# One chunk a turn by single-row DMAs, shared between SyncE and ScalarE; one-hots and a bias addition moved on VectorE

## What is computed

```python
# 6250 nodes x 256; 106250 edges sorted by target (17 per node on average)
x = x + gnn(layernorm(x))      # graph layer, LSTM-like cell, projection
x = x + ffn(layernorm(x))      # slice attention over all nodes

# gnn(z):
agg = segment_sum(z[src], dst)                       # the gather and the sum over edges
h = relu(agg @ W_rel + b_rel + z @ W_root)           # 256 -> 512
i, f, g, o = split(h @ W_ih.T + b_ih + b_hh, 4)      # 512 -> 2048, f unused
c = sigmoid(i) * tanh(g)
return (sigmoid(o) * tanh(c)) @ W_fc + b_fc          # 512 -> 256

# ffn(z): weights = softmax((z @ W_x + b_x) @ W_slice ...) per head,
# tokens = weights^T (z @ W_fx), attention among the 64 tokens of a head,
# then weights @ tokens and W_out for every node
```

## Time and profile before

| | before |
|---|---|
| median of 3 runs | 1237.53 us (1236.96 to 1239.23) |
| profiled execution | 1240.34 us, of which span 1238.5 us |
| PE busy, share of span | 1116.1 us, 90% |
| DVE | 831.8 us, 67% |
| POOL | 805.3 us, 65% |
| ACT | 627.2 us, 51% |
| granted PE clock, mean | 0.994 |

### The profile page before, as it was taken

How to read it: one execution, slowest core, us unless ns; L and a number is a source line. 1 busy time by engine, 2 the same in 40 slices (tenths; PEclk the granted TensorE clock), 3 DMA queues, 4 the chain that set the end, 5 groups by cost and what they waited for, 6 DMA issues and landing times. The chain is left out here.

```text
span 1238.5 us, 30254 instructions
## 1 busy us (share of the span) xinstructions
PE 1116.1 (90%) x9821; PEld 967.1 (78%) x9821; DVE 831.8 (67%) x2560; ACT 627.2 (51%) x1257; POOL 805.3 (65%) x856
## 2 busy tenths in 40 slices
PE   1077799999999999999999999999999999999998
PEld 0046688878888888788888787888888878897798
DVE  7885476667666766676677756775767566746665
ACT  5872444554456454545554545455545454555332
POOL 5877777777777777777777777777777777400000
PEclk9998999999999999999999999999999999999999
DMA  8674444444454445444544444444444454313498
GB/s 313 225 268 119 125 130 136 147 142 136 129 148 142 141 124 150 140 140 123 150 149 138 121 148 150 137 121 150 147 136 122 150 149 137 97 44 116 129 336 290
DMA packets 92966, 188.74 MB, mean 152 GB/s; under 512 B 20914, under 2 KB 55591, under 8 KB 92821
## 3 DMA queue, kind: packets, MB, share of 16 engines
q0 software_dynamic: 39168, 107.01, 30.0%
q1 hardware_dynamic: 42794, 59.89, 14.8%
q10 hardware_dynamic: 10859, 20.05, 4.5%
HBM read 154.87 MB, written 32.00 MB: 151 GB/s over the span
## 5 line engine op out<-in xcount | busy, mean ns | idle before, releaser
L700 POOL DMA_INDIRECT ring<-table,sidx x798 | 763.5, 957 | 247.5 <-issue 242.7
L419 PE MATMUL ps<-h_h,wih_h 128*128 128x250 f32 x1200 | 338.8, 282 | 0.0
L420 PE MATMUL ps<-h_l,wih_h 128*128 128x250 f32 x1200 | 336.5, 280 | 0.0
L421 PE MATMUL ps<-h_h,wih_l 128*128 128x250 f32 x1200 | 336.5, 280 | 0.0
L419 PEld LDWEIGHTS ps<-h_h,wih_h 128*128 128x128 f32 x1200 | 230.1, 192 | 2.0 <-issue 0.8
L420 PEld LDWEIGHTS ps<-h_l,wih_h 128*128 128x128 f32 x1200 | 230.2, 192 | 1.1
L421 PEld LDWEIGHTS ps<-h_h,wih_l 128*128 128x128 f32 x1200 | 230.1, 192 | 0.0
L850 ACT ACTIVATE gate<-ps,bgate 128x250 f32<-128x250 f32 x300 | 124.2, 467 | 140.7 <-PE ps L421 139.7
L651 DVE TENSOR_SCALAR oneh<-iota,didx 128x64 f16<-128x64 f16 (+2 forms) x1179 | 183.1, 259 | 0.0
L1078 PE MATMUL ps<-ring,oneh 128*32 128x512 f16 x2280 | 151.0, 391 | 34.5 <-DMA ring<-table,sidx 31.9
L1078 PEld LDWEIGHTS ps<-ring,oneh 128*32 128x32 f16 x2280 | 59.5, 97 | 107.7 <-DMA ring<-table,sidx 46.4
(11 more groups left out here) (213 smaller groups left out, 2508.4 us busy)
## 6 DMA issues: line engine op xcount, KB each, us to landing
sp_ring<-table SPq DMA_DIRECT2D x1920, 1.0 KB
ring<-table,sidx POOLq DMA_INDIRECT x798
swt_d<-swt ACTq DMA_DIRECT2D x25, 500.0 KB
gate<-swt_d SPq DMA_DIRECT2D x19, 500.0 KB, 5.9
x_room<-in_x SPq DMA_DIRECT2D x12, 512.0 KB, 10.6
xn<-table SPq DMA_DIRECT2D x25, 224.0 KB
xin<-in_x SPq DMA_DIRECT2D x25, 224.0 KB
res<-xin SPq DMA_DIRECT2D x25, 224.0 KB
```

The lines of the kernel that those rows point to most:

```text
L419: eng.matmul(dst, wh, xh, start=first, stop=False)
L420: eng.matmul(dst, wh, xl, start=False, stop=False)
L421: return eng.matmul(dst, wl, xh, start=False, stop=last)
L700: pool.indirect_dma_start(ring[:, j, :], None, table, bass.IndirectOffsetOnAxis(ap=idx, axis=0)).then_inc(done, 16)
```

## The change

- `SP_STEP` 52 to 33 and `SP_N` 15 to 23: chunks 86, 119, ..., 812 are fetched row by row, one a turn; GpSimd's list has 8 chunks less.
- Of such a chunk's 128 rows SP issues 88 (8, 16 and 64 a turn, 88 in turn 0; addresses in loads of 22) and ACT 40 (20 in turn 0, then 40 a turn in steady state; addresses in loads of 10). Each of the two waits for the slot and the addresses itself; PE waits for all 128 rows as before.
- ACT's rows stand at eleven places of its turn; its turns are written out one by one, no longer a hardware loop.
- DVE's one-hots for block 2t+2 are written half in turn t, where all stood, and half in turn t+1, between the statistics of `norm_x2` and the reciprocal (the new `scale_x2`).
- `add_bfc` stands right after the one-hots of block 2t+1, ahead of `cell_c` 0.

```diff
-    SP_FIRST, SP_STEP, SP_N, SP_SLOTS = 86, 52, 15, 3
+    SP_FIRST, SP_STEP, SP_N, SP_SLOTS = 86, 33, 23, 3
...
-    ROWS_FIRST, ROWS, LOADS = 96, (8, 16, 60), 32
+    ROWS_FIRST, ROWS, LOADS = 88, (8, 16, 64), 22
+    SP_ROWS = 4 * LOADS
+    ACT_ROWS = P - SP_ROWS
+    ACT_FIRST, ACT_LOADS = 20, 10
...
+        def wait_slot(eng, k):
+            if k == 0:
+                eng.wait_ge(spi_done, 1)
+            if k >= SP_SLOTS:
+                b = last_reader(SP_CHUNKS[k - SP_SLOTS])
+                eng.wait_ge(sum_done[b % 2], b // 2 + 1)
+                eng.wait_ge(sum_done[(b - 1) % 2], (b - 1) // 2 + 1)
+
+        def load_starts(eng, k, q, n):
+            _, at = nc.values_load_multi_w_load_instructions(
+                sp_idx[k:k + 1, q:q + n], engines=[eng.engine], min_val=0, max_val=(N - 1) * row_bytes,
+                skip_runtime_bounds_check_because="the DMA checks its bounds")
+            return at
+
+        def fetch_row(eng, k, q, start):
+            to = sp_ring[q:q + 1, k % SP_SLOTS, :].bitcast(U8)
+            eng.dma_start(to, rows8[ds(start, row_bytes)].rearrange("(p c) -> p c", p=1)).then_inc(
+                sp_rows[k % SP_SLOTS], 16)
...
-        def hots(eng, b):
+        def hots(eng, b, part=None):
...
+            half = len(plan) // 2
+            chunks = list(plan.items())[(part or 0) * half:half if part == 0 else len(plan)]
+            if part != 1:
+                after(eng, sum_done[e], b // 2)
...
-            last.then_inc(hot_done[e], 1)
+            if part != 0:
+                last.then_inc(hot_done[e], 1)
...
+            def load_rows():
+
+                r = loaded[0]
+                if r < last_row and r < row_at[0] + ACT_LOADS:
+                    k, q = r // ACT_ROWS, r % ACT_ROWS
+                    if q == 0:
+                        wait_slot(act, k)
+                    for i, start in enumerate(load_starts(act, k, SP_ROWS + q, ACT_LOADS)):
+                        starts[r + i] = start
+                    loaded[0] += ACT_LOADS
+
+            def fetch_rows(n):
+
+                for r in range(row_at[0], min(row_at[0] + n, loaded[0])):
+                    fetch_row(act, r // ACT_ROWS, SP_ROWS + r % ACT_ROWS, starts.pop(r))
+                    row_at[0] += 1
+
             def turn(t, odd, gather, gnn, ffn, ahead):
+                if t == 0:
+                    for _ in range(ACT_FIRST // ACT_LOADS):
+                        load_rows()
+                        fetch_rows(ACT_LOADS)
                 if gnn:
                     split_x(t - 1)
+                    load_rows()
+                    fetch_rows(9)
                     relu_h(t - 1, 0)
...
-                    gates(t - 1, 0, 4)
+                    fetch_rows(2)
+                    gates(t - 1, 0, 2)
+                    load_rows()
+                    fetch_rows(1)
+                    gates(t - 1, 2, 4)
                     tanh_c(t - 1, 0)
+                    load_rows()
+                    fetch_rows(9)
...
-                    gates(t - 1, 4, 8)
+                    gates(t - 1, 4, 6)
+                    fetch_rows(1)
+                    gates(t - 1, 6, 8)
                     tanh_c(t - 1, 1)
+                    fetch_rows(4)
                     gates(t - 1, 8, 10)
+                    load_rows()
+                    fetch_rows(3)
...
                     gates(t - 1, 10, 12)
+                    fetch_rows(1)
                     high_hl(t - 1, 0)
+                    fetch_rows(1)
                     tanh_c(t - 1, 3)
...
+                    fetch_rows(1)
                     high_hl(t - 1, 1)
...
                                   swt[:, :, :, :].rearrange("p e j n -> p (e j n)")).then_inc(swt_st, 16)
+                    fetch_rows(9)
...
-            with act.Fori(lo, hi, step) as t:
+            for t in range(lo, hi, step):
...
                     norm_x2(t - 2)
+                    if gather:
+                        hots(dve, 2 * t, 1)
+                    scale_x2(t - 2)
...
                 if gather and gnn:
                     hots(dve, 2 * t + 1)
                 if gnn:
+                    add_bfc(t - 1)
+                if gnn:
                     cell_c(t - 1, 0)
...
                 if ahead:
-                    hots(dve, 2 * t + 2)
+                    hots(dve, 2 * t + 2, 0 if t else None)
...
-                if gnn:
-                    add_bfc(t - 1)
```

More of the change, by code:

```diff
@@ L438, in out_count @@
             return 16 * (len(range(q, NCH + 1, TILES)) + (len(REST_PARTS) - 1 if q == NCH % TILES else 0))
+        rows8 = table.bitcast(U8).rearrange("n c -> (n c)")
+        row_bytes = 4 * C
+        def wait_slot(eng, k):
[14 more added lines that the diff above has]
+                sp_rows[k % SP_SLOTS], 16)
         @block.sync
@@ L517, in _ @@
             row_at = [0]
-            rows8 = table.bitcast(U8).rearrange("n c -> (n c)")
-            row_bytes = 4 * C
             def fetch_rows(n):
-                for r in range(row_at[0], min(row_at[0] + n, SP_N * P)):
-                    k, q = r // P, r % P
+                for r in range(row_at[0], min(row_at[0] + n, SP_N * SP_ROWS)):
+                    k, q = r // SP_ROWS, r % SP_ROWS
                     if q == 0:
[L526 to L531, removed]
-                    if q % LOADS == 0:
[L533 to L539, removed]
+                        wait_slot(sp, k)
+                    if q % LOADS == 0:
+                        starts[:] = load_starts(sp, k, q, LOADS)
+                    fetch_row(sp, k, q, starts[q % LOADS])
                 row_at[0] += n
@@ L548, in turn @@
                     for j, k in SP_OF.items():
-                        assert first_reader(j) // 2 > t or row_at[0] >= (k + 1) * P, (t, j, k, row_at)
+                        assert first_reader(j) // 2 > t or row_at[0] >= (k + 1) * SP_ROWS, (t, j, k, row_at)
                 if gather:
@@ L579, in _ @@
             last_turns(turn)
-            assert row_at[0] >= SP_N * P
+            assert row_at[0] >= SP_N * SP_ROWS
             def f_load(n, k):
@@ L642, in ln_low @@
                               ALU.subtract).then_inc(ln_lo[q], 1)
-        def hots(eng, b):
+        def hots(eng, b, part=None):
             e, (plan, _) = b % 2, hot_plan(b)
-            after(eng, sum_done[e], b // 2)
-            for j, (w0, w1, at) in plan.items():
+            half = len(plan) // 2
+            chunks = list(plan.items())[(part or 0) * half:half if part == 0 else len(plan)]
+            if part != 1:
+                after(eng, sum_done[e], b // 2)
+            for j, (w0, w1, at) in chunks:
                 n = WIN * (w1 - w0)
@@ L873, in copy_out @@
                                ACT.Copy).then_inc(att_a, 1)
-            def turn(t, odd, gather, gnn, ffn, ahead):
+            row_at, loaded, starts = [0], [0], {}
+            last_row = SP_N * ACT_ROWS
+            def load_rows():
[11 more added lines that the diff above has]
+                    row_at[0] += 1
+            def turn(t, odd, gather, gnn, ffn, ahead):
+                if gather and t < NP - 1:
+                    for j, k in SP_OF.items():
+                        assert first_reader(j) // 2 > t or row_at[0] >= (k + 1) * ACT_ROWS, (t, j, k, row_at)
+                if t == 0:
+                    for _ in range(ACT_FIRST // ACT_LOADS):
+                        load_rows()
+                        fetch_rows(ACT_LOADS)
                 if gnn:
                     split_x(t - 1)
+                    load_rows()
+                    fetch_rows(9)
                     relu_h(t - 1, 0)
@@ L936, in _ @@
             lo, hi, step = turns(turn)
-            with act.Fori(lo, hi, step) as t:
+            for t in range(lo, hi, step):
                 two_turns(turn, t)
             last_turns(turn)
+            assert row_at[0] == last_row
             def f_high(n, k):
@@ L1545, in norm_x2, with scale_x2 @@
                     dve.bn_aggr(mv[0:WN, 0, e, :], stats[0:WN, 0, e, :]).then_inc(var_done, 1)
+            def scale_x2(p):
                 dve.wait_ge(sd_done, p + 1)
```

## The result

The changed kernel takes **1363.46 us** (median of 4 runs, 1362.18 to 1369.3) against 1237.37 us before: a ratio of **1.1025**, 95% interval 1.0999 to 1.1051. It is 126 us slower, where 11.2 us of gain were forecast. The profiled execution took 1369.3 us around a span of 1367.5 us; its mean granted TensorE clock is 0.955 (0.994 before).

What follows compares the result with a forecast made beforehand. GpSimd's back-to-back gathers were taken as the bound, at 1.263 us each. Nine fewer before block 48 save 11.4, less up to 0.4 in the last turns: 11.2 off 1237.53 gives 1226.3 us, between 1223.5 and 1229 (chance 0.66).

Steps and rivals of the forecast that it cites:

- the price of an address load: SyncE's and ACT's register loads: between 2.13 for 32 and 0.486 for one, 22 take 1.60 and 10 take 0.96.
- The "hidden" of SyncE's 2.1 us: SyncE's queue: rows +1.3 and loads +0.8 a turn, hidden in its 4.6 us wait at L555 for the next turn.
- TensorE (B): TensorE becomes the bound as ACT's covers spill, some gain left: 1230.5, range 1229 to 1236; chance 0.14.
- contention of issuers (C): Rows issued by SyncE and ACT go one after the other: 1250; decides from ACT pitch of some 0.48; chance 0.12.
- slower gathers (D): Additional rows slow GpSimd's gathers; 1.4% (0.018 us) eats the 11.4 us, time 1235 to 1240; chance 0.08.
- The slower side: Chance that the kernel measures slower than before: 0.11, contention of issuers (C) less its edge.
- Fewer gathers, nine times 1.263: GpSimd's list: block 48 waits for the 777th gather instead of the 786th, 11.4 us less if TensorE keeps up.
- TensorE's turn of 39.3 to 40.0: TensorE's own turn: 39.28 to 39.99, taken as 39.6, under GpSimd's supply of 40.65 us a turn.
- ACT's rows: ACT's turn: 16.6 us more of rows and loads, mostly hidden in its waits; up to +0.36 a turn for TensorE.
- the last place: ACT's 9 rows behind the store: split_x 1.65 late, 1.29 covered; up to +0.36 us, nothing if the store moves ahead.
- Half of the one-hots: VectorE before softmax_end: it begins 1.9 earlier, TensorE's 0.68 wait at L1155 shrinks by 0.33 to 0.68 a turn.
- b_fc sooner, 0 to 0.3: VectorE before cell_c: 0.76 us put in a 0.84 wait, now waiting for the x load; costs 0 to 0.3.

Runs made afterwards that it cites:

- e1_aligned: The change with same rows and places, but address loads all beginning at multiples of four registers (SyncE 20, 24, 20, 24; ACT 12, 8, 12, 8): 1231.76 us, ratio 0.9942.
- e8_whole_onehots: Against e1_aligned: all one-hots of block 2t+2 written in turn t again, b_fc still added early: 1235.25 us.
- e9_rows_alone: Against e1_aligned: both VectorE edits undone (one-hots whole, b_fc at its old place), so only the rows are new: 1231.71 us.
- e2_sp_aligned: Against the change: only SyncE's loads moved to multiples of four (20, 24, 20, 24), ACT's left at 10 each: 1243.52 us, ratio 1.0036.

## Why the prediction was wrong, step by step

- **The step that failed** is the price of an address load: "on a line between, 22 take 1.60 and 10 take 0.96". The line was drawn through the number of registers. The row for 32 and the one for a single register are both of loads that begin at a multiple of four, so the trace held no load of the other kind, and two rows of one kind were taken for the bounds of both. Half of the new loads are of the other kind: 4.87 instead of 1.60. (The others were 0.25 to 0.32 too low as well, for their length; all four at 1.85 to 1.92 would still have been hidden.) SyncE's loads grew by 13.5 - 5.6 = 7.9 us a turn, not by 0.8; with 1.3 for the rows that is 9.2 against the 4.6 of slack. 41.1 + 9.2 - 4.6 = 45.7 would be the turn; 46.7 was measured, the other 1.0 in the rows and the gaps between them (30.8, where before they took 41.1 - 4.6 - 5.6 - 2.5 = 28.4 and 1.3 were to come). The kernel before showed only loads from a multiple of four on (2.13 for 32), which made 22 look cheap. The Trainium skill, Runtime: NRT & Kernel Launch, "Instruction fetch mechanics", gives some 200 ns a register for a TENSOR_LOAD, even in bulk. It speaks of loads that the runtime puts in; of these loads from SBUF, those from 2 on agree (0.200), those from a multiple of four on don't (0.056).
- **The "hidden" of SyncE's 2.1 us** stood on that price. The slack itself was read rightly, as the turn just worked out shows to within 1.0.
- **Which engine could become the bound.** The rivals had TensorE (B), contention of issuers (C) and slower gathers (D), none SyncE itself, though its slack was one subtraction away. The slower side was given 0.11 for a mechanism that the rows don't show: ACT's beside SyncE's take 0.34 to 0.37 each (9 in 3.10 to 3.36 us), far from the 0.48 from which C decides. Rival D's price had a slip: 0.018 us more a gather are 14 us over 777 gathers; 0.0147 (1.2%) would eat the 11.4.

```profile
660.15 3.36 ACTq L462 DMA_DIRECT2D sp_ring<-table  x9
...
666.17 3.10 ACTq L462 DMA_DIRECT2D sp_ring<-table  x9
```

- **Fewer gathers, nine times 1.263.** Right in kind, as e1_aligned shows. The chain again goes from GpSimd to TensorE at block 48:

```profile
1044.20 0.94 POOL ring L719
...
1045.45 2.74 DMA ring<-table,sidx
...
1048.23 0.61 PE ps L1143 x7
```

  The 777th gather is issued at 1045.45, 7.9 us before the 786th of before. Nine gathers are 11.4; the first starts 1.7 earlier (60.59); and 776 gathers at 1.2692 instead of 1.2626 cost 5.1, rival D on a small scale. Part of these 5.1 may be no effect of the change, as profiles with the gathers of the kernel before range from 1.263 to 1.269. With aligned loads the forecast was right save for this term: 7 to 8 us of gain where 11.2 were forecast.
- **TensorE's turn of 39.3 to 40.0.** Right for aligned loads: TensorE's stalls for gathers, 37.6 us in 25 places, remain in a mean turn of 40.8.
- **ACT's rows** were covered place by place as said once the loads were short: TensorE's wait for the last split is 3.2 us in all. It was the earlier store, from the halved one-hots, that covered the last place, as the step said: with whole one-hots this wait is 14.4 in 22 places (e8_whole_onehots) and 9.3 in 20 (e9_rows_alone). With 3.7 us a turn more on ACT the covers do not hold (e2_sp_aligned); they were as thin as rival B had them.
- **Half of the one-hots**: right (1.3 in 2 places instead of 16.3 in 24).
- **b_fc sooner, 0 to 0.3.** Right with aligned loads as to the wait: VectorE waits for the x load only once at the start and once at the end (5.4 us in 2 places). In the change itself the new place costs 27.5, as the load is late. What the step left out is what the two additions do to a gather in their new place.

## What to carry to other kernels

Price a moved or resized instruction from rows of its own kind, and where its place in memory changes with its size, count the place as part of the kind: an interpolation over size alone between two rows of one alignment bounds nothing. A queue that is off the critical path has a slack that can be read, one wait a turn; put next to it the dearest price the edit could have, and give the engine that would then set the turn a chance of its own. Address lists that are loaded to registers in pieces are best cut so that every piece begins at a multiple of four registers and has a multiple of four in it.

## What the runs showed of the hardware

- A load of consecutive 32-bit registers from SBUF took 0.056 us a register where it began at a multiple of four (16 bytes) and 0.200 where it didn't, on SyncE (22: 1.87 to 1.89 against 4.72 to 4.73); on ACT, 10 registers took 1.18 and 2.39. A load that began two registers off kept to 0.200 up to its last register (32 from 2 on: 6.73). With a length that is no multiple of four it was dearer than the next longer one that is: 22 took 1.85 to 1.92, 24 took 1.72.
- Rows issued by ACT beside SyncE's came 0.33 us apart (median), SyncE's 0.322 as before; at this rate two issuers cost each other next to nothing.
- GpSimd's indirect DMA, 0.95 us, took up to 1.60 beside two VectorE additions with both operands in SBUF, and the ones beside no VectorE instruction 0.946 on average.
